# A DLRM tower on one core: own orders of steps for the first two pairs of tiles, a replanned steady order, and the last layer in four column groups

## What is computed

```python
e = stack([tbl_f[ids[:, f]] for f in range(32)], axis=1)        # (2048, 32, 64)
z = einsum('bne,hne,bnh->bn', e[:, ROW], kernel, e[:, COL])     # kernel (64, 496, 64)
h = concatenate([z, dense_ctx], axis=1)                         # (2048, 512)
h = maximum(h @ W_top1 + b_top1, 0)                             # 512 -> 512
h = maximum(h @ W_top2 + b_top2, 0)                             # 512 -> 256
y = h @ W_top3                                                  # 256 -> 1
```

## Time and profile before

| | us |
|---|---|
| median of 3 runs | 790.78 (790.67 to 790.79) |
| span of the profiled execution | 789.1 |
| PE busy | 737.3 (93%) |
| ACT busy | 707.2 (90%) |
| DVE busy | 699.8 (89%) |
| POOL busy | 553.3 (70%) |
| mean granted TensorE clock | 0.994 |

### The profile page before, as it was taken

The page is one execution under the profiler, slowest core; times in us unless marked ns, Lnnn a source line. Parts: engine busy times, 40 slices in busy tenths (PEclk is TensorE's granted clock), DMA queues, the critical chain, the costliest instruction groups (busy, mean ns, idle before and its releaser), DMA issues.

```text
span 789.1 us, 18454 instructions
## 1 busy us (share of the span) xinstructions
PE 737.3 (93%) x5352; PEld 450.9 (57%) x5352; DVE 699.8 (89%) x680; ACT 707.2 (90%) x5517; POOL 553.3 (70%) x578
## 2 busy tenths in 40 slices
PE   2668888899999999999999999999999999999998
PEld 1444545556566565666566565666566665665656
DVE  1368988899999899999999999999999999998993
ACT  0367898989999999999999999999999999999994
POOL 6777777777777777777777777787778777781110
PEclk9989999999999999999999999999999999999999
DMA  1556311111111111111111111111111111110000
GB/s 35 152 167 175 107 27 28 28 25 25 25 27 25 26 23 25 26 25 24 25 24 25 25 25 25 25 24 26 23 27 25 25 25 24 26 25 1 2 1 0
DMA packets 33141, 28.09 MB, mean 36 GB/s; under 512 B 19720, under 2 KB 20752, under 8 KB 33040
## 3 DMA queue, kind: packets, MB, share of 16 engines
q0 software_dynamic: 16384, 16.81, 11.1%
q1 hardware_dynamic: 16656, 10.11, 4.7%
HBM read 26.87 MB, written 0.01 MB: 34 GB/s over the span
## 4 chain that ended last, share of the span: by engine, by line
PE 82%; POOL 5%; DVE 5%; issue 4%; ACT 2%; DMA 1%; DVEq 0%; POOLq 0%
PE T L656 33%; PE T L644 20%; PE psZ L676 11%; PE psE L605 11%; POOL E_low L388 5%; PE psE L590 4%; ACT prod L456 2%; DVE z L552 2%; DVE prod L527 2%; DVE prod_t L506 1%; PE psZ L600 1%; PE T L692 1%; DMA E_low<-tbl,idx 1%; PE psE L692 0%; DVE prod L524 0%
## 5 line engine op out<-in xcount | busy, mean ns | idle before, releaser
L456 ACT ACTIVATE prod<-prod 128x64 f32<-128x64 f32 x2688 | 642.3, 242 | 16.0 <-DVE prod L524 6.4
L456 ACT ACTIVATION_READ_ACCUMULATOR prod<-prod 128x1 f32 x2688 | 507.0, 189 | 0.0
L656 PE MATMUL T<-kst,eT 64*128 64x512 f32 (+3 forms) x2304 | 335.5, 418 | 8.9 <-issue 4.1
L388 POOL DMA_INDIRECT E_low<-tbl,idx x256 | 242.0, 945 | 85.3 <-issue 56.2
L388 POOL DMA_INDIRECT E_high<-tbl,idx x256 | 241.9, 945 | 77.6 <-issue 53.0
L506 DVE TENSOR_TENSOR prod_t<-T,eT 128x1024 f32<-128x1024 f32 x192 | 232.2, 1216 | 25.4 <-PE T L644 25.4
L524 DVE TENSOR_TENSOR prod<-T,E_low 128x1024 f32<-128x1024 f32 x192 | 231.4, 1217 | 14.4 <-PE T L656 12.7
L656 PEld LDWEIGHTS T<-kst,eT 64*128 64x128 f32 x2304 | 180.0, 190 | 97.1 <-issue 44.6
L644 PE MATMUL T<-eT,kst 64*128 64x256 f32 x1536 | 206.4, 392 | 13.8 <-ACT eT L431 7.4
L644 PEld LDWEIGHTS T<-eT,kst 64*128 64x128 f32 x1536 | 145.0, 190 | 81.9 <-issue 45.6
L552 DVE TENSOR_REDUCE z<-prod 128x16 f32<-128x1024 f32 (+7 forms) x161 | 135.6, 870 | 1.7 <-POOL prod L398 1.7
(11 more groups left out here) (42 smaller groups left out, 203.4 us busy)
## 6 DMA issues: line engine op xcount, KB each, us to landing
kst<-K_T SPq DMA_DIRECT2D x28, 256.0 KB, 3.0
E_low<-tbl,idx POOLq DMA_INDIRECT x256, 2.4
E_high<-tbl,idx POOLq DMA_INDIRECT x256, 2.4
w<-W_top SPq DMA_DIRECT2D x1, 1024.0 KB
kst<-K_T SPq DMA_DIRECT2D x4, 192.0 KB, 4.6
w<-W_top SPq DMA_DIRECT2D x1, 512.0 KB
z<-dense_ctx SPq DMA_DIRECT2D x16, 8.0 KB
idx<-ids SPq DMA_DIRECT2D x1, 224.0 KB, 4.5
```

The source lines that it names most:

```text
L388: nc.gpsimd.indirect_dma_start(out=embeddings(t, b, g)[:, f % GF, :], out_offset=None, in_=tables[f], in_offset=bass.IndirectOffsetOnAxis( ...
L456: last = nc.scalar.activation(x, x, ACT.Copy, accum_out=z[:, b, Z_COLUMNS[s][m]:Z_COLUMNS[s][m] + 1])
L656: last = nc.tensor.matmul(T[:, s_ring(t, n), bank + m * D:bank + (m + w) * D], eT[rows, i // 2, b * P:(b + 1) * P], kst[rows, at + m * D:a ...
```

## The change

Pairs 0 and 1 get orders of their own over the 64 steps (`FIRST`, `SECOND`, as positions in the new `ORDER`), pairs 2 to 7 the new `ORDER`. In pair 0 the transposes are 27 units (`FIRST_UNITS`: first stack, number of stacks, tiles), most of one stack of one tile; gathers and loads of `kst` follow their order. Steps of bursts, transposes and layers are listed anew for each, and so are the places of ACT's copies, now as (step, accumulations done in it), so that a copy can stand inside a step's accumulations. `DVE_SHARE` has an entry for each slot; halving starts in pair 2 with 6 pairs of steps; reductions have a lag each. The last layer runs in four column groups of PE, 64 of the 256 columns each, right ahead of a burst in the next pair; y is 4 partitions of 64 for a pair.

```diff
-ORDER = ("f00 f00 t01 s00 t01 s00 c01 c01 c01 c01 t01 t01 f11 s11 t02 f11",
-         "t02 s11 c12 t12 c12 t12 c02 c02 c02 t12 c02 t02 t12 c12 t02 c12",
-         "f22 s22 f22 t23 t23 s22 c03 c03 t13 c03 t23 c03 t23 t13 c13 c13",
-         "c03 t13 c03 t13 t23 c03 t23 c03 c13 c13 t23 f33 t23 s33 s33 f33")
+ORDER = ("t01 t01 c01 t01 f00 f00 f11 s11 t02 s11 c12 c12 t02 t12 f11 c01",
+         "c02 c02 s22 f22 t12 c01 c01 t12 s00 t12 s00 c02 c02 t02 t01 c12",
+         "c12 t02 c03 t23 c03 f33 t13 t13 f33 f22 t13 c03 t23 c03 s22 s33",
+         "s33 t23 t23 c03 t23 c03 t23 c13 c13 t13 t23 c03 c03 t23 c13 c13")
-DVE_SHARE = {"cross": 6, "first": 8, "second": 8}
-HALVED_SHARE = {15: 7, 26: 7, 19: 5, 11: 5, 9: 5, 4: 8}
-HALVED = (1, 3, 5, 7, 10, 13, 15, 18)
-HALVED_FROM = 1
+FIRST = (15, 60, 22, 5, 26, 63, 9, 14, 30, 24, 4, 3, 0, 17, 21, 1, 7, 6, 13, 2, 16, 27, 23, 25, 28, 8, 12, 11, 10, 46, 29, 19, 33,
+         32, 20, 31, 41, 57, 18, 42, 34, 52, 47, 40, 37, 59, 61, 39, 56, 48, 38, 58, 44, 36, 43, 54, 45, 55, 49, 50, 62, 53, 51,
+         35)
+FIRST_UNITS = ((6, 1, '0'), (5, 1, '1'), (15, 1, '1'), (3, 1, '1'), (7, 1, '1'), (2, 1, '1'), (0, 1, '1'), (1, 1, '1'), (3, 1, '0'),
+               (6, 1, '1'), (4, 1, '1'), (2, 1, '0'), (0, 2, '0'), (4, 1, '0'), (9, 1, '1'), (7, 1, '0'), (5, 1, '0'), (9, 1, '0'),
+               (10, 1, '0'), (10, 1, '1'), (8, 1, '01'), (11, 1, '01'), (13, 1, '1'), (13, 1, '0'), (14, 2, '0'), (12, 1, '01'),
+               (14, 1, '1'))
+FIRST_BURST_STEP = (21, 32, 46, 52, 64, 66)
+FIRST_LEAD = 3
+SECOND = (4, 5, 26, 24, 1, 3, 0, 9, 21, 22, 15, 7, 2, 14, 6, 30, 20, 8, 25, 10, 27, 32, 31, 28, 29, 46, 18, 11, 16, 23, 33, 12, 56,
+          40, 17, 59, 13, 54, 47, 51, 41, 50, 19, 58, 36, 52, 55, 38, 43, 61, 45, 44, 39, 35, 57, 42, 53, 60, 49, 34, 48, 63, 62,
+          37)
+SECOND_TR_STEP = (-8, -3, 4, 5, 17, 18, 29, 30)
+SECOND_BURST_STEP = (23, 29, 41, 49, 58, 68)
+DVE_SHARE = (4, 8, 5, 8, 8, 8, 2, 4, 3, 7, 6, 6, 8, 5, 8, 8, 4, 10, 5, 3, 7, 7, 5, 6, 5, 4, 10, 6, 9, 3, 2, 11)
+HALVED = (10, 14, 15, 16, 17, 19)
+HALVED_FROM = 2
 HALVED_LAST = (1, 2, 3, 5, 6, 7, 9, 10, 12, 15, 16, 17)
-TR_STEP = (-13, -10, -7, -3, 6, 8, 24, 27)
-Z_STEP = (41, 69)
-MLP_STEP = {('l1', 0): 76, ('l1', 1): 81, ('l1', 2): 86, ('l1', 3): 95, ('l2', 0): 99, ('l2', 1): 107, ('l3', 0): 111}
+TR_STEP = (-12, -9, -1, 0, 6, 16, 29, 30)
+TR_OUT = ((-15, 6), (-15, 6), (-4, 1), (-3, 5), (5, 2), (13, 3), (23, 8), (23, 8))
+BURST_STEP = (12, 29, 41, 52, 59, 71)
+Z_OUT = ((38, 10), (70, 1))
+MLP_STEP = {('l1', 0): 76, ('l1', 1): 83, ('l1', 2): 87, ('l1', 3): 97, ('l2', 0): 101, ('l2', 1): 109}
+MLP_OUT = {('l1', 0): (77, 3), ('l1', 1): (81, 1), ('l1', 2): (87, 8), ('l1', 3): (92, 1), ('l2', 0): (101, 10), ('l2', 1): (106, 7)}
+L3_BURST = 4
+SCORE_OUT = (59, 5)
+REDUCE_LAG = (1, 5, 1, 1, 2, 5, 7, 2, 5, 7, 6, 4, 5, 6, 5, 9, 6, 6, 8, 4)
...
+        uses.append((NS * (t + 1) + BURSTS_AT[t + 1][L3_BURST], "l3", t, 0))
...
-            for f in range(GF):
-                gather(0, 0, 0, f)
...
+            for m, (some, bs) in enumerate(UNITS[0]):
+                for x in some:
+                    for b in bs:
+                        for f in (2 * x, 2 * x + 1):
+                            gather(0, f // GF, b, f % GF)
...
-                for m in range(share(t, n), SIZE[s]):
+                for k, m in enumerate(range(share(n), SIZE[s])):
+                    if k > 0:
+                        outs(when(t, n), k)
...
+            def last_layer(o, k, q):
+                cols = slice(q * 2 * P // QUADS, (q + 1) * 2 * P // QUADS)
+                return nc.tensor.matmul(o[q * QUAD:q * QUAD + 1, 0:2 * P // QUADS], w3[:, k:k + 1], h2T[:, k, cols], start=(k == 0), stop=(k == M2 - 1))
...
-                return layer(o[0:1], lambda k: w3[:, k:k + 1], h2T[:, :, :], M2)
+                for k in range(M2):
+                    for q in range(QUADS):
+                        last = last_layer(o, k, q)
+                return last
...
             for at in range(STEPS):
-                products(at // NS, at % NS)
+                products(at // NS, SEQ[at // NS][at % NS])
+                for n, *use in uses_at.get(at, []):
+                    if use[0] == "l3":
+                        use_bank(n, *use)
                 if at in burst_at and at < STEPS - 1:
                     sum_burst(*burst_at[at])
                 for n, *use in uses_at.get(at, []):
-                    use_bank(n, *use)
+                    if use[0] != "l3":
+                        use_bank(n, *use)
```

More of the change, by code:

```diff
@@ L153, in dlrm_tower, with stacks_of @@
[L153 to L160, removed]
+    def stacks_of(n):
+        (kind, g, h, a), b = of[n], ORDERED[n][1]
+        if kind == "turned":
+            return {(GS * g + 2 * b + y, x) for y in (0, 1) for x in (0, 1)}, {(GS * h + a, x) for x in (0, 1)}
+        return {(GS * h + x, b) for x in ((a,) if kind == "cross" else range(GS))}, set()
@@ L187, in reduces_of @@
[L187 to L191, removed]
+        t, n = divmod(n, NU)
+        return sum(map(len, REDUCES[:t])) + sum(UPRIGHT[t].index(some[0]) < n for some in (REDUCES[t] if t < PAIRS else []))
@@ L196, in dlrm_tower @@
     for q in range(PASSES):
-        t, half = divmod(q, 2)
+        t = q // 2
         for n in range(bursts):
[L199 to L203, removed]
+            last = when(t, own(q)[BURST * n + BURST - 1])
+            at = NS * t + BURSTS_AT[t][q % 2 * bursts + n]
+            if (q, n) == (PASSES - 1, bursts - 1):
+                at = last + LAST_SUM_LAG
+            assert at > last and at not in burst_at
@@ L221, in dlrm_tower, with units_of @@
[L221 to L224, removed]
+    assert all(sorted((x, b) for some, bs in units for x in some for b in bs) == [(x, b) for x in range(STACKS) for b in (0, 1)] for units in UNITS)
+    def units_of(t, n, part):
+        need = stacks_of(n)[part]
+        return max((ordinal["tr", t, m] for m, (some, bs) in enumerate(UNITS[t]) if need & {(x, b) for x in some for b in bs}), default=-1) + 1
@@ L225, in dlrm_tower @@
+    uses, latest = [], NS
+    for m, (some, bs) in reversed(list(enumerate(UNITS[0]))):
+        have = {(x, b) for x in some for b in bs}
+        latest = min([latest] + [at - 1 for at, n in enumerate(FIRST) if any(part & have for part in stacks_of(n))])
+        uses.append((latest, "tr", 0, m))
+    uses.reverse()
     for t in range(1, PAIRS):
         for m in range(len(UNITS[t])):
-            uses.append((NS * t + TR_STEP[m], "tr", t, m))
+            uses.append((NS * t + TR_AT[t][m], "tr", t, m))
@@ new lines, in _ @@
+            latest = (STEPS, 0)
+            for n, (at, what, t, m) in reversed(list(enumerate(uses))):
+                if what == "tr":
+                    step, k = (SECOND_TR_OUT if t == 1 else TR_OUT)[m] if t > 0 else (max(-1, at - FIRST_LEAD), 0)
+                    where = (NS * t + step, k)
+                elif what == "l3":
+                    where = (NS * (t + 1) + SCORE_OUT[0], SCORE_OUT[1])
+                else:
+                    where = (LAST_OUT if t == PAIRS - 2 else MLP_OUT)[what, m]
+                    where = (NS * t + where[0], where[1])
+                latest = min(latest, where)
+                outs_at.setdefault(latest, []).insert(0, ("bank", n, what, t, m))
@@ L730, in _ @@
                     pe.wait_ge(tail_act, 4)
-                last = nc.tensor.matmul(L3_OUT[0:1], w3[:, k:k + 1], h2T[:, k, :], start=(k == 0), stop=(k == M2 - 1))
+                for q in range(QUADS):
+                    last = last_layer(L3_OUT, k, q)
             last.then_inc(tail_pe, 1)
```

262 lines of the change are left out of this document (150 added, 112 removed).

## The result

The changed kernel takes 777.01 us (median of 4 runs, 775.73 to 777.41) against 790.78: a ratio of 0.9823 with the 95% interval [0.9809, 0.9837], 13.8 us less where 28.7 were forecast. Its profiled execution has a span of 775.0 us.

The account below looks back on a forecast made before the run. PE was taken as the bound, ACT and DVE close behind. Pairs 0 and 1 end at 213.8, + 1.0 + 5 x 88.4 + 88.6 + 15.0 = 760.4 of span, with 1.7 outside 762.1 us; range 756 to 778.

Parts of the forecast that it names:

- The steady pair: Pairs 2 to 7: PE and DVE level at 87.2 us of work, plus 1.2 of waits, 88.4 a pair.
- rival of a steady pair that gives little: Steady pairs: DVE waits for POOL's late halves, 90.4 us a pair and 774 in all; chance 0.17.
- The last layer: On PE: four column groups run side by side and take 0.25 us instead of 0.95.
- rival that the groups don't run side by side: On PE: the grouped last layer still takes 0.95 us, 767 in all; chance 0.10.
- Pair 0: First pair: level with the gathers throughout, 2.3 us over their bound, ending at 121.5 instead of 135.6.
- a burst 1.85: PE's price for each burst of 16 matmuls, read from the trace before: 1.85 us.
- the bound by gathers: Pair 0's earliest end: a position's gather + 2.4 + 2.7 + DVE's work from there on; 119.2 us at position 14.
- rival of a pair 0 as ragged as before: Pair 0 ends 14 us over its bound, at 133.2, and the kernel takes 771; chance 0.15.
- Pair 1: Second pair: held by POOL's gathers, ending at 213.8 us instead of 228.7.
- the bound by the 128th gather: Pair 1: that gather lands at 164.2 us, transposes after step 29 wait for it, so the pair ends at 213.3.
- Last pair and tail: End of the kernel: last pair 88.6 us, 0.2 over the other steady pairs, then 15.0 as before.
- Slower by ACT standing at its copies: Steady pairs: ACT arrives early at copies inside its accumulations and stands, 95.5 us a pair, 804 in all; chance 0.04.

Follow-up runs that it names:

- uneven4: `rows` with another permutation of the rows: pairs 0 and 1 stay even, four of six steady bursts get three products of one parity; 789.49 us.
- flat: The changed kernel with its last layer ungrouped again, two matmuls over all 256 columns, still ahead of its burst; 780.37 us.
- before_groups: The kernel before the change with only the last layer in four column groups, and y's copy and store in that form; 787.15 us.
- rows: The changed kernel with the turned products' rows in psZ permuted so that every burst has two of each parity; 769.63 us.
- second_steady: `rows` with pair 1 in the steady order and its lists, while pair 0 keeps its own order; 781.89 us.

## Why the prediction was right and wrong

The runs split the 13.8 us: groups 3.6 (790.8 to 787.2), the steady order planned anew 5.0 (to 782.2, pair 1 no longer halved in it), own orders 12.6 (to 769.6), and uneven bursts take 7.4 back (to 777.0).

- **The steady pair: right, 88.45 for 88.4**, but by luck, as two errors cancel. I summed DVE's work to 87.2 from prices of single instructions; it is 88.1. PE's sum was 87.2 too; PE is at work for 88.3, and by `uneven4` and `flat` it sets the pair. Had I added the 1.5 that the change brings to the 86.69 of the earlier trace rows, I would have had 88.2. And DVE's waits are 0.4, not 1.2. The rival of a steady pair that gives little falls: no halving is waited for in pairs 3 to 6.
- **The last layer: right.** 0.22 us, and the rival that the groups don't run side by side falls. The Trainium skill's section Instruction Overhead (page TensorEngine Tiling (Array Packing)) would have made it an estimated 0.4; the trace disagrees, 16 matmul rows of 64 columns over four groups start 14 ns apart on average (0.22/16), and between two products, in `before_groups`, they cost 0.33.
- **Pair 0: 127.1 for 121.5.** The step that failed is "a burst 1.85" for all of them. I took the price from steady bursts and used it for orders that deal rows to column groups in another way. That is 3.2 of 5.6. The other 2.4 remain in `rows`: DVE's work is 92.0, not 90.6, and 7.5 us of waits stand for the 6.5 implied. Of the 1.4 of work, 0.4 is that two steps with unequal shares are reduced one by one (26 reductions for the 20 of the sum, at its 0.06 each); the rest is about the shortfall that the sum has in a steady pair (0.9). Of the 7.5 us of waits, 5.4 are six waits for T between 33 and 52 us, in and around a stretch in which PE works at the lower clock (before it, from 20 us on, PE had been at work for 1.4, 4.3 and 3.9 of each 5 us). I had priced transposes and products there as in the steady part. Windows of `rows`:

```profile
core 0: us, PE busy (x) PEld busy (x) DVE busy (x) ACT busy (x) POOL busy (x), PEclk, DMA share, GB/s
35.00:40.00 5.00, 4.23 (x17) 2.07 (x13) 3.33 (x4) 2.65 (x23) 3.78 (x5) 0.50 0.33 80
40.00:45.00 5.00, 4.53 (x29) 3.91 (x30) 2.80 (x4) 4.43 (x35) 3.78 (x5) 0.50 0.31 82
```

  How much of the waits the clock makes was not tested. Nothing ends sooner than the bound by gathers allowed, and the rival of a pair 0 as ragged as before (133.2) falls.
- **Pair 1: 98.5 for 92.3.** Uneven bursts are 3.2 of 6.2 here too. Of the other 3.0, 1.1 is DVE's work (32 reductions for the 20 of the sum; 91.7 us for 90.6), the rest waits that I didn't count. PE never waited for a gather at 164, as I said it would: it came there later than the bound. So the bound by the 128th gather is neither shown nor refuted. That POOL's rate can bind pair 1 is shown by `second_steady`, at the 96th and 112th gather.
- **Pair 2: 89.9 for 89.4**: 0.9 of it is the uneven burst at its start, where I had 1.0 for a gather.
- **Last pair and tail: 2.0 more than said.** The last pair has DVE waits of 4.9 us, 1.0 of them for a halving by POOL and 0.9 for psZ; I had taken it as a steady one plus 0.2. No run tests it.
- **Slower by ACT standing at its copies: falls.** ACT is idle for 4.5 us in a steady pair, and none of DVE's waits there names ACT.

So the step that failed is the price of a burst, put at 1.85 us whatever order its products come in, where nine of the twelve in pairs 0 and 1 take 2.70 or 3.56. That is half of the miss: the changed kernel is 14.9 us from the forecast, with even rows 7.5. The other half are smaller terms: DVE's work and waits in pairs 0 and 1, and the last pair with the tail. No duration in the trace of before could show the long bursts; the row arithmetic in the code, applied to `FIRST` and `SECOND`, would have.

The best kernel here is `rows`, 769.63 us, which beats both: 2.7% under before and 7.4 us under the changed one.

## What to carry to other kernels

A price read from a steady part holds for the assignment of resources there; when an order changes, work out again which column group each instruction gets, since an uneven deal can nearly double the same instructions. Speeding up one stage against a fixed-rate supplier brings nothing unless the next stage also asks for less early on: of two orders that are worth 12.6 us together, the first was worth nothing alone. And the two waits of nearly 6 us there cost more than their length, as PE worked at the lower clock behind them. On an engine that executes in order, price what stands ahead of a moved instruction as well as what it puts off.

## What the runs showed that I had not expected

- The same 16 matmuls of 512 columns take 1.85 us where they fill the four column groups evenly, 2.70 at three to one, and 3.56 on two of the groups alone. The time follows the fuller side: 2, 3 or 4 products at 0.85 each, and 0.15 beside.
- An ungrouped last layer and the burst behind it overlap on PE: together they take 2.67 us, not 0.95 + 1.85. Whether that takes different column groups is not shown; no run varies it.
- After waits of 5.8 and 5.7 us PE's granted clock was 0.50, and the 3.0 and 3.4 us of work behind them took about 1.5 us too long each (`second_steady`).
- One addition of 0.6 us on POOL cost DVE 12.0 us of waiting, as its reduction stood one step behind the product.
